# Routing of a gated mixture on one Trainium2 core: GpSimd's powers replaced by ScalarE's tanh, and the first block's routing spread out

## The reference

```python
logits = h2 @ router_w                      # 4096 tokens x 8 experts
probs = softmax(logits, axis=-1)
topw, topi = top_k(probs, 2)
topw = softmax(topw, axis=-1)
combine = sum(one_hot(topi, 8) * topw[..., None], axis=1)
shared = swiglu(h2, sh_gate, sh_up, sh_down)
gate = einsum('td,edf->etf', h2, e_gate); up = einsum('td,edf->etf', h2, e_up)
eout = einsum('etf,efd->etd', silu(gate) * up, e_down)
out = X + shared + einsum('etd,te->td', eout, combine)
```

## Time and profile before

| | |
|---|---|
| median of 3 runs | 1391.35 us (1389.79 to 1395.53) |
| profiled execution | 1394.36 us, span 1392.6 us |
| TensorE, VectorE busy | 1125.4 us (81%), 1023.8 us (74%) |
| ScalarE, GpSimd busy | 822.9 us (59%), 726.4 us (52%) |
| gated layer | about 508.7 to 866.9 us of the span |
| mean granted TensorE clock | 0.891 of full speed |

### The profile page before, as it was taken

How to read it: one execution, slowest core, us unless ns; L and a number is a source line. 1 busy time by engine, 2 the same in 40 slices (tenths; PEclk the granted TensorE clock), 3 DMA queues, 4 the chain that set the end, 5 groups by cost and what they waited for, 6 DMA issues and landing times. The chain is left out here.

```text
span 1392.6 us, 33039 instructions
## 1 busy us (share of the span) xinstructions
PE 1125.4 (81%) x11620; PEld 632.5 (45%) x11620; DVE 1023.8 (74%) x2724; ACT 822.9 (59%) x1693; POOL 726.4 (52%) x711
## 2 busy tenths in 40 slices
PE   2879999999999968898898987699999995505740
PEld 1334444444444435454555554355555553503540
DVE  2779999999999816877778777359999995482117
ACT  0568888888888845454555544368888882101303
POOL 3124444553324116666676666358888885205645
PEclk9989999999999979999999999559999995556975
DMA  4231111111111100000000000001111100431125
GB/s 102 62 90 27 33 29 31 31 31 31 33 30 35 26 1 1 1 1 1 1 1 1 1 1 1 26 25 28 29 28 29 32 22 31 152 106 31 42 77 138
DMA packets 78881, 48.80 MB, mean 35 GB/s; under 512 B 12855, under 2 KB 75776, under 8 KB 78720
## 3 DMA queue, kind: packets, MB, share of 16 engines
q1 hardware_dynamic: 76928, 43.02, 11.3%
q0 software_dynamic: 1792, 3.67, 0.9%
HBM read 16.48 MB, written 10.22 MB: 19 GB/s over the span
## 5 line engine op out<-in xcount | busy, mean ns | idle before, releaser
L487 DVE TENSOR_REDUCE mxsS<-scoreS 128x2 f32<-128x512 f32 x512 | 328.9, 685 | 42.6 <-PE scoreS L593 37.6
L385 ACT ACTIVATE PTS<-stS 128x512 f32<-128x512 f32 x512 | 283.5, 591 | 58.5 <-PE stS L597 58.2
L1748 POOL TENSOR_TENSOR ghid<-gprod,ghid 128x512 f16<-128x512 f32 x144 | 164.7, 1157 | 112.5 <-ACT ghid L1846 111.9
L593 PE MATMUL scoreS<-QK 31*128 31x256 f16 x1024 | 171.6, 281 | 27.9 <-DVE mxsS L487 12.5
L775 POOL TENSOR_TENSOR PTP<-PTP,EP 128x512 f32<-128x512 f32 x128 | 162.4, 1277 | 60.1 <-ACT PTP L907 60.1
L597 PE MATMUL stS<-QK 32*128 32x256 f16 x1024 | 168.0, 278 | 1.3 <-ACT PTS L385 1.3
L1846 ACT ACTIVATE ghid<-gprod 128x512 f16<-128x512 f32 x144 | 90.1, 625 | 131.4 <-DVE gprod L1925 131.3
L613 PE MATMUL pvS<-PTS,Vx 128*32 128x256 f32 x2048 | 142.2, 397 | 0.1
L1023 DVE TENSOR_SCALAR AP<-score_psP 128x768 int32<-128x768 int32 x128 | 121.5, 950 | 25.4 <-PE score_psP L1130 25.1
L1796 PE MATMUL up_ps<-ghT,split 128*128 128x512 f16 x432 | 120.3, 388 | 19.7 <-DVE gprod L1925 19.6
L907 ACT ACTIVATE PTP<-AP,epsP 128x768 f32<-128x768 f32 x128 | 119.2, 931 | 14.2 <-DVE AP L1023 14.1
(11 more groups left out here) (301 smaller groups left out, 2276.1 us busy)
## 6 DMA issues: line engine op xcount, KB each, us to landing
QK<-HLS SPq DMA_DIRECT2D x384, 32.0 KB, 1.9
QK<-HLP SPq DMA_DIRECT2D x192, 32.0 KB, 1.9
expert_outputs<-rzero SPq DMA_DIRECT2D x8, 512.0 KB, 3.2
cgot<-expert_outputs SPq DMA_DIRECT2D x16, 256.0 KB, 5.1
X<-in_L_attn_x_dram SPq DMA_DIRECT2D x4, 512.0 KB
tokens<-ry SPq DMA_DIRECT2D x8, 256.0 KB, 2.3
out_dram<-X SPq DMA_DIRECT2D x8, 256.0 KB, 2.3
wi<-L_ffn_experts_inter_dram SPq DMA_DIRECT2D x1, 1792.0 KB, 8.0
```

What stands on the lines that cost most here:

```text
L385: act.activation(PT[:, n % NPT, :], st_ps[:, (NS * t + n) % 3, :], ACT.Exp, scale=SCALE).then_inc(s_exp, 1)
L487: dve.tensor_reduce(mxs[:, u // 4, :, at], score_ps[:, n % 2, :].rearrange("p (c s) -> p c s", c=TC), AX.X, ALU.max).then_inc(s_max, 1)
L593: scored = pe.matmul(score_ps[:, k, cols], QK[part, new, g, 0, rows], QK[part, new, g, 1, :], start=True, stop=True)
L1748: pool.tensor_tensor(hid[:, n // FC % NHID, 1, c, :], prod[:, n % NPROD, :], hid[:, n // FC % NHID, 0, c, :], ALU.subtract).then_inc(s_hid, 1)
```

## The change

The top two experts are now picked on the shifted logits l - max instead of the probabilities; ties are settled as before by `pri`. The exponentials are no longer powers on GpSimd. ScalarE computes th = tanh((l - max)/2), and VectorE makes e to the power of l - max from it as 2/(1 - th) - 1. The softmax over the two probabilities is made from tanh of half of their difference, since its weights are (1 + tanh)/2 and (1 - tanh)/2. GpSimd keeps only its reciprocal square roots, and its fill of `base` goes.

VectorE has 27 routing steps instead of 25, in six parts: 4 at q = 13, 5 at q = 14, 4 at q = 15, 5 at q = 16 (this part waits for the first tanh), 4 at q = 17, and 5 at q = 2 of the block itself (these wait for the second tanh). ScalarE's tanh calls stand at the end of q = 14 and of q = 1.

Block 0 is placed differently: only its part 0 runs ahead of product(0). Its first tanh is at q = 1, parts 1 to 4 follow product(1) to product(4), the second tanh is at q = 5, and part 5 follows product(6), ahead of the first add.

```diff
@@ gpsimd
-            def exponentials(t):
-                pool.wait_ge(s_route, ROUTE * t + EXP0)
-                pool.tensor_tensor(pr[:], base[:], pr[:], ALU.pow).then_inc(s_exp, 1)
-
-            def second_exponential(t):
-                pool.wait_ge(s_route, ROUTE * t + EXP1)
-                pool.tensor_tensor(one[:], base[:, :, 0], one[:], ALU.pow).then_inc(s_exp, 1)
...
-                    if q == 14 and has(t + 1):
-                        exponentials(t + 1)
-                    if q == 1 and has(t):
-                        second_exponential(t)
@@ scalar
+            def tanh_of_logits(t):
+                act.wait_ge(s_route, ROUTE * t + SHIFTED)
+                act.activation(th[:], pr[:], ACT.Tanh, scale=0.5).then_inc(s_tanh, 1)
+
+            def tanh_of_spread(t):
+                act.wait_ge(s_route, ROUTE * t + SPREAD_OF)
+                act.activation(two[:], one[:], ACT.Tanh, scale=0.5).then_inc(s_tanh, 1)
...
+                    if q == 14 and has(t + 1) and t + 1 > 0:
+                        tanh_of_logits(t + 1)
+                    if q == 1 and t == 0:
+                        tanh_of_logits(t)
+                    if q == 1 and has(t) and t > 0:
+                        tanh_of_spread(t)
+                    if q == 5 and t == 0:
+                        tanh_of_spread(t)
@@ vector, route(t, part)
-                    lk(dve.tensor_reduce(one[:], lg[:], AX.X, ALU.max))
-                    lk(dve.tensor_tensor(pr[:], lg[:], wide(one[:]), ALU.subtract))
+                    lk(dve.tensor_reduce(m[:, 0, :], lg[:], AX.X, ALU.max))
+                    lk(dve.tensor_tensor(pr[:], lg[:], wide(m[:, 0, :]), ALU.subtract))
+                    lk(dve.tensor_scalar(sc[:], pr[:], 0.0, None, ALU.is_equal))
...
+                elif part == 3:
+                    dve.wait_ge(s_tanh, 2 * t + 1)
+                    lk.skip_to(13)
+                    lk(dve.tensor_scalar(odds[:], th[:], -1.0, 1.0, ALU.mult, ALU.add))
+                    lk(dve.reciprocal(odds[:], odds[:]))
+                    lk(dve.tensor_scalar(odds[:], odds[:], 2.0, -1.0, ALU.mult, ALU.add))
+                    lk(dve.tensor_tensor(sc[:], odds[:], sel[:, 1, :, :], ALU.mult))
+                    lk(dve.tensor_reduce(total[:], odds[:], AX.X, ALU.add))
+                elif part == 4:
+                    lk.skip_to(18)
+                    lk(dve.tensor_reduce(one[:], sc[:], AX.X, ALU.add))
+                    lk(dve.tensor_scalar(one[:], one[:], -1.0, 1.0, ALU.mult, ALU.add))
+                    lk(dve.reciprocal(total[:], total[:]))
+                    lk(dve.tensor_tensor(one[:], one[:], total[:], ALU.mult))
                 else:
-                    dve.wait_ge(s_exp, 2 * t + 2)
+                    dve.wait_ge(s_tanh, 2 * t + 2)
...
@@ vector, the loop
+                    if 1 <= q < 5 and t == 0:
+                        route(t, q)
+                    if q == 6 and t == 0:
+                        route(t, 5)
...
-                    if q in (13, 15, 16, 17) and has(t + 1):
-                        route(t + 1, (13, 15, 16, 17).index(q))
-                    if q == 2 and has(t):
-                        route(t, 4)
+                    if q == 13 and has(t + 1):
+                        route(t + 1, 0)
+                    if 13 < q < 18 and has(t + 1) and t + 1 > 0:
+                        route(t + 1, q - 13)
+                    if q == 2 and has(t) and t > 0:
+                        route(t, 5)
```

More of the change, by code:

```diff
@@ L1663, in gated_layer @@
         sc = sb("sc", c8)
-        base = sb("base", c8)
+        th = sb("th", c8)
+        odds = sb("odds", c8)
         sel = sb("sel", [P, 2, TB, NE])
@@ L1668, in gated_layer @@
         two = sb("two", [P, TB])
+        total = sb("total", [P, TB])
         comb = sb("comb", [P, 2, TB, NE])
@@ L1693, in gated_layer @@
         s_route = sem("s_route")
-        s_exp = sem("s_exp")
+        s_tanh = sem("s_tanh")
         s_gate = sem("s_gate")
@@ L1707, in gated_layer @@
         block = ctx.enter_context(nc.Block())
-        ROUTE, EXP0, EXP1 = 25, 3, 18
+        ROUTE, SHIFTED, SPREAD_OF = 27, 3, 22
         def has(t):
@@ L1723, in _ @@
             pool.memset(half[:], -0.5).then_inc(s_half, 1)
-            pool.memset(base[:], float(np.exp(1.0))).then_inc(s_half, 1)
-            pool.wait_ge(s_half, 2)
+            pool.wait_ge(s_half, 1)
             def in_root(t):
@@ L1880, in route @@
                 pri = cst[:, C_PRI:C_PRI + NE].unsqueeze(1).to_broadcast(c8)
+                lk = Link(dve, s_route, ROUTE, t)
                 if part == 0:
                     dve.wait_ge(s_logits, t + 1)
[L1883 removed]
                     lk(dve.tensor_scalar(lg[:].rearrange("p c e -> p (c e)"), turn_ps[:, 0:TB * NE], 1.0 / LIFT, None,
                                          ALU.mult))
[L1886 removed]
@@ L1887, in route @@
-                    lk(dve.tensor_tensor(pr[:], lg[:], wide(one[:]), ALU.subtract))
+                    lk(dve.tensor_reduce(m[:, 0, :], lg[:], AX.X, ALU.max))
+                    lk(dve.tensor_tensor(pr[:], lg[:], wide(m[:, 0, :]), ALU.subtract))
+                    lk(dve.tensor_scalar(sc[:], pr[:], 0.0, None, ALU.is_equal))
                 elif part == 1:
-                    dve.wait_ge(s_exp, 2 * t + 1)
-                    lk = Link(dve, s_route, ROUTE, t).skip_to(EXP0)
-                    lk(dve.tensor_reduce(one[:], pr[:], AX.X, ALU.add))
@@ L1892, in route @@
[L1892 to L1899, removed]
+                    lk.skip_to(4)
@@ L1900, in route @@
                     lk(dve.tensor_tensor(sc[:], sc[:], pri, ALU.mult))
                     lk(dve.tensor_reduce(two[:], sc[:], AX.X, ALU.max))
[L1902 to L1908, removed]
+                    lk(dve.tensor_tensor(sel[:, 0, :, :], sc[:], wide(two[:]), ALU.is_equal))
@@ new lines, in route @@
+                    lk(dve.scalar_tensor_tensor(p2[:].rearrange("p t e -> p (t e)"),
+                                                sel[:, 0, :, :].rearrange("p t e -> p (t e)"), MASKED,
+                                                pr[:].rearrange("p t e -> p (t e)"), ALU.mult, ALU.add))
+                    lk(dve.tensor_reduce(m[:, 1, :], p2[:], AX.X, ALU.max))
+                elif part == 2:
+                    lk.skip_to(9)
+                    lk(dve.tensor_tensor(sc[:], p2[:], wide(m[:, 1, :]), ALU.is_equal))
+                    lk(dve.tensor_tensor(sc[:], sc[:], pri, ALU.mult))
+                    lk(dve.tensor_reduce(two[:], sc[:], AX.X, ALU.max))
+                    lk(dve.tensor_tensor(sel[:, 1, :, :], sc[:], wide(two[:]), ALU.is_equal))
+                elif part == 3:
[12 more added lines that the diff above has]
+                    lk(dve.tensor_tensor(one[:], one[:], total[:], ALU.mult))
@@ L1909, in route @@
                 else:
-                    dve.wait_ge(s_exp, 2 * t + 2)
+                    dve.wait_ge(s_tanh, 2 * t + 2)
                     reach(dve, s_acc, EX * (t - 1))
[L1912 to L1916, removed]
+                    lk.skip_to(22)
@@ L1917, in route @@
+                    half_of = 0.5 * LIFT ** -2
+                    lk(dve.tensor_scalar(m[:, 0, :], two[:], half_of, half_of, ALU.mult, ALU.add))
+                    lk(dve.tensor_scalar(m[:, 1, :], two[:], -half_of, half_of, ALU.mult, ALU.add))
                     lk(dve.tensor_tensor(sc[:], sel[:, 0, :, :], wide(m[:, 0, :]), ALU.mult))
```

## The result

The changed kernel is faster: a median of 1339.9 us in four runs (1332.4 to 1344.3) against 1393.3 us, a ratio of 0.961 with a 95% interval of 0.956 to 0.966. Two later sets of runs gave 0.966 (0.961 to 0.971) and 0.963 (0.960 to 0.966).

A forecast was written before the change was run, and what follows sets the result against it. VectorE's wait for GpSimd's power was taken to delay products that TensorE needs. Steady blocks 21 us plus first block 6 us made 27 off the profiled 1394.4, and less 3.0 for the median about 1364.5 us, range 1354 to 1388.

The forecast's parts named there:

- So a block loses 4.58 us to the routing: In a steady block, gate(18) to gate(26): TensorE loses 3.70 plus 0.88 us to the next block's routing.
- 10.4 us for the low half of `hT`, which this change leaves alone: TensorE's wait in the gated layer for the low half of hT, 10.4 us, claimed untouched by the change.
- 32 us is all that can be won there: Over seven blocks of the gated layer, 7 x 4.58 us claimed as the most that could be won.
- beside that for `pr` I count on no wait for GpSimd in the earlier trace: Gated layer: no wait for GpSimd counted except VectorE's for the power, 38.1 us, eight times.
- I take 3.0 of 4.58.: Seven steady blocks: 3.0 of 4.58 us won in each, 21 us in all, bounds 14 and 32.
- The first walk: One later block without waits for GpSimd: product(21) ends at 654.8, needed by 655.55; all 4.58 us won.
- The second: Same block with GpSimd waits of 0.9, 0.6, 0.7 and 0.5 us in four parts: 2.0 to 2.6 us won.
- One sign set for being wrong: Routing steps behind products 14 to 17 lasting over 1.9 us a part would show the forecast wrong.
- The 6 us: Block 0, routing spread between products: 6 us won, bounds 4.5 and 6.5; gate(8) at 531.6 to 533.
- The table is not reloaded: Rival: Tanh not readable from Silu's table, four loads, 5.13 us of ScalarE a block; 1398 us, chance 0.17.
- VectorE did not stay the bound: Rival: VectorE's two-input steps wait for GpSimd's low in every part; 1385.5 or 1381 us, chance 0.12.
- All of it, and the clock too: Rival: no wait left and no slow clock stretch in the opening; 1351 us, chance 0.05.

The follow-up runs named there:

- late_power: Changed kernel with the eight exponentials made by GpSimd's power again, at unit 14 and asked for at unit 16; gated layer 337.6 us, ratio 0.978 to the kernel before.
- exp_table: Changed kernel with ScalarE's exponential, from another table than Silu, in place of the first tanh; gated layer 337.3 us, ratio 0.985 to the kernel before.
- lump: Changed kernel with parts 1 to 4 of later blocks' routing in one piece behind product(17); gated layer 330.8 us, ratio 0.968 to the kernel before.
- Old_order_tanh: Kernel before with both powers replaced by a tanh on ScalarE, 25 steps and old order kept; gated layer 323.1 us, ratio 0.976 to the kernel before.
- root_early: As no_spread, with GpSimd's reciprocal root at unit 7 instead of 8; gated layer 306.1 us, ratio 0.959, again 0.957, to the kernel before.
- no_spread: Changed kernel with the first block's routing ahead of its first product again; gated layer 313.5 us, ratio 0.963 to the kernel before.
- spread_only: Kernel before, powers and 25 steps kept, only the first block's routing moved between its products; gated layer 359.2 us, ratio 0.995 to the kernel before.
- low_early: As no_spread, with the low half of hT made behind product(9) instead of product(10); gated layer 314.9 us, ratio 0.967 to the kernel before.
- before_again: The kernel before once more, unaltered; one run, 1390.8 us, gated layer 362.6 us.
- pad_reduce: Changed kernel with two idle one-input reductions more ahead of each of parts 1 to 4; gated layer 343.8 us, ratio 0.984 to the kernel before.
- pad_two: Changed kernel with two idle two-input steps more ahead of each of parts 1 to 4; gated layer 344.0 us, ratio 0.983 to the kernel before.

## Why the prediction was wrong

*What bounds the kernel.* Right in kind: the path ran through VectorE's wait for the power. The size of what could be won was wrong. "So a block loses 4.58 us to the routing" stopped counting at gate(26). But product(21) was still late there, and that lateness went on through ScalarE. Its queue holds, behind high(21), Silu 23, high(22), the four scalings of the next block's tokens and Silu 24, and product(24) waits for that last one. Timeline of the kernel before, from product(21) at 659.43 to the transposes at 663.97 and past them:

```profile
661.69 1.26 ACT L1829 ACTIVATE gy<-XB,girs 128x128 f32<-128x128 f32 x4
...
662.86 0.58 ACT L1840 ACTIVATE gsg<-gate_ps 128x512 f32<-128x512 f32 x1
...
663.47 0.69 DVE L1925 TENSOR_TENSOR gprod<-gsg,up_ps 128x512 f32<-128x512 f32 x1 [1.36 <-ACT gsg L1840]
...
666.53 1.28 DVE L1925 TENSOR_TENSOR gprod<-gsg,up_ps 128x512 f32<-128x512 f32 x2
```

And of the changed kernel, from product(21) at 637.66 to the transposes at 643.00 and past them:

```profile
641.09 0.58 ACT L1837 ACTIVATE gsg<-gate_ps 128x512 f32<-128x512 f32 x1
...
641.70 0.69 DVE L1938 TENSOR_TENSOR gprod<-gsg,up_ps 128x512 f32<-128x512 f32 x1 [1.36 <-ACT gsg L1837]
...
644.76 1.28 DVE L1938 TENSOR_TENSOR gprod<-gsg,up_ps 128x512 f32<-128x512 f32 x2
```

In both, Silu 24 starts 3.43 us after product(21), VectorE stands 1.36 us for it, and product(7) of the next block follows 7.10 us after product(21). Against the transposes it comes at 2.56 us before and at 1.76 after. Those 0.8 us reach, over the normalisation, the waits ahead of up(12) (0.36 and its overlap, now none) and of the logits (1.47, now 1.18). The step that failed is "10.4 us for the low half of `hT`, which this change leaves alone" (it fell to 9.0), and with it "32 us is all that can be won there": it was 5.4 a block. Every kernel in which product(21) was late had the old 0.36 and 1.47 again: late_power, exp_table, lump and both pads. Old_order_tanh had them too, with product(21) 1.8 us later in the block than in the changed kernel, though TensorE had no stall for it. And each of the three profiles of the changed kernel has one block in which product(21) is 0.3 us late against the transposes that follow; the next wait for the logits is 1.47 us, and that block lasts 37.8. So the 0.75 us that the walk had "in hand" at product(21) were not free.

Another reading was wrong: "beside that for `pr` I count on no wait for GpSimd in the earlier trace rows". The same answer has this row; the changed kernel still has 9.7 us of it:

```profile
DVE gtmp L1952 <- POOL grs L1735: 10.0, 8, 1.3
```

It lies between the transposes and the logits of each later block, and root_early shows what it is worth: 1.23 us a block.

*"I take 3.0 of 4.58."* This term was the larger miss: 21 us forecast, and what seven blocks gave without the clock is 34.0 (2.38 + 31.6). The first walk, which let nothing wait for GpSimd, hit product(21) within 0.1 us, in part by luck: product(18) ended 1.15 us later after gate(18) than walked, which the idle time walked ahead of product(20) and shorter moments (1.68 us for the 2.05) made up. The second, with 2.7 us of such waits, did not come about. The steps did wait, 0.6 + 0.8 us in parts 1 to 4, half of what I had put in, and the old 2.05 us for the moments held a wait of the same kind (0.63 for a step of 0.17), which went. I had counted one kind of collision where it would appear and not where it would vanish. One sign set for being wrong did come, a part of over 1.9 us (part 3, from 627.60, lasts 2.03), and cost nothing there.

The rule of the Trainium skill that I weighed (GPSIMD Engine Reference, Key points) agrees with the trace for one-input scalings too: they took 0.98 to 1.14 us beside a `low` (L1912, L1928). That they ran in the mode with two ports, no row shows. But the conclusion that the sum would lie nearer to 14 us was wrong, as fewer of them met one.

*The first block.* The 6 us were right (6.16), as the time at which gate(8) comes. What failed was the tail of that walk, which let no step wait for GpSimd. It had the first add end at 534.1, in time for down(2), which TensorE reaches 2.75 us after gate(8), walked at 531.6 to 533. Four steps of block 0 waited 3.6 us in all (those in part 5 are shown above), and the add ended 27.7 us after the layer's first instruction where the walk had 25.4. Either half of the change brings the 6 us alone: no_spread's opening is 5.7 us shorter than before, spread_only's 6.0, but only the spreading gives some back.

*The clock.* The sum had no term for it in the later blocks. There the two profiles of the kernel before have two and four spells of some 3.4 us at half the clock, each in the first products behind the stall ahead of the logits, at 1.67 us. Timeline of TensorE in late_power, where it is the same:

```profile
624.88 0.46 PE L1777 MATMUL gturn_ps<-router,ghT 128*128 128x8 f16 x12 [1.47 <-DVE ghT L1884]
625.20 1.44 PE L1788 MATMUL gate_ps<-ghT,split 128*128 128x512 f16 x3
...
626.43 1.49 PE L1793 MATMUL up_ps<-ghT,split 128*128 128x512 f16 x3
```

In the later blocks such spells came in eight of the nine profiles whose stall there is 1.47 us each time, and in none of the seven where it is usually 1.18 us or less (three of the changed kernel, in which one stall of seven is 1.47, no_spread, low_early, root_early twice). That is a pattern in 16 profiles; no run here separates the length of that stall from the other idle time that goes with it. It is 3.3 us of this profile and up to 6.7 against before_again.

*The rivals.* The table is not reloaded: Tanh needed no load behind Silu. My price for it was wrong too, since exp_table gave 2.1 us for a pair where I had 0.3 at unit 14. VectorE did not stay the bound; pad_reduce and pad_two show that it is close by. "All of it, and the clock too", at 0.05 the least likely, was nearest, and still too small.

*What stays open.* The median fell by 53 us in the first set and by 47 and 53 in the later two, with 43.5 to 47.1 in the gated layer's profiles. The rest fits the power layer's changing clock (292 to 310 us in 16 profiles, with no relation to the kernel that I can see), but what decides when the clock rises in that layer was not tried.

## What to carry to other kernels

A lateness doesn't end where its last visible stall ends, nor where the late engine next stands idle: here it passed through ScalarE's queue and came back while VectorE waited. Follow it until every engine has its input in time, and count each later stall before that as its price. When the removal of a wait shifts two engines that hinder each other, walk the new order once with and once without the hindrance, and check which collisions of the *old* order vanish before leaning to the pessimistic walk. And split a change that has two ideas: here the exchange of engines brought 4.4 us a block, the new order 1.0, spreading out the first block cost 2, and the next gain was a 1 us instruction moved by one place.

## What the runs showed of the hardware

A short VectorE scaling with one SBUF input lasted until GpSimd's current `low` ended, as a step with two does: three in a row took 1.12, 1.08 and 1.08 us for 0.18 beside three `low`s without a pause. Reductions beside a `low` took their 0.17 to 0.19 us in all 16 profiles. GpSimd's 5.4 us power, in late_power, held up no VectorE step (two-input steps of 0.18 and 0.19 us ran during it). Two ACT_TABLE_LOADs of 1.283 us with a 0.23 us exponential between them took 2.84 us in all. A short reciprocal of 32 values took 0.35 us, one of 4 values 0.18.
